# Order of products, activations and additions in the last convolutions of a four-block kernel

## What is computed

```python
def _L3_conv_ref(x, Wq, Wk, Wv, Wc, gamma, beta):
    q, k, v = conv3x3(x, Wq), conv3x3(x, Wk), conv3x3(x, Wv)
    att = softmax(einsum('nchw,mchw->nmhw', q, k) / sqrt(C), axis=1)
    virt = einsum('nmhw,mchw->nchw', att, v)
    mu, var = mean(virt, axis=(1, 2, 3)), var(virt, axis=(1, 2, 3))
    virt = (virt - mu) * rsqrt(var + 1e-05)
    virt = relu(virt * gamma + beta)
    return x + conv3x3(virt, Wc)
```

## Time and profile before

| | |
|---|---|
| Median of 3 executions | 482.8 us (481.6 to 485.68) |
| The profiled execution | 482.77 us, its span 481.0 us |
| Busy share of the span | PE 94%, DVE 71%, ACT 53%, POOL 26% |
| Granted TensorE clock, mean | 0.988 |
| Chain that ended last | PE 73%, DVE 10%, ACT 10%, issue 4%, DMA 2%, POOL 1% |

### The profile page before, as it was taken

How to read it: one execution, slowest core, us unless ns; L and a number is a source line. 1 busy time by engine, 2 the same in 40 slices (tenths; PEclk the granted TensorE clock), 3 DMA queues, 4 the chain that set the end, 5 groups by cost and what they waited for, 6 DMA issues and landing times.

```text
span 481.0 us, 10582 instructions
## 1 busy us (share of the span) xinstructions
PE 451.1 (94%) x3792; PEld 371.5 (77%) x3792; DVE 340.9 (71%) x891; ACT 254.6 (53%) x607; POOL 124.8 (26%) x154
## 2 busy tenths in 40 slices
PE   8898999899999999999999999999988999987995
PEld 7677775677887787778778877778766799887995
DVE  1567557976977897788778868986585344775995
ACT  4516737655646556575556565554654520494551
POOL 6115800351121012111210210121042011423662
PEclk9999999999999999999999999999995999999999
DMA  7210200030010001000200000000000000005111
GB/s 278 57 63 2 72 23 0 2 115 4 1 44 24 1 1 44 22 0 0 65 0 0 22 0 0 1 24 1 0 23 1 1 24 1 1 1 174 46 64 67
DMA packets 10639, 15.28 MB, mean 32 GB/s; under 512 B 624, under 2 KB 8944, under 8 KB 10480
## 3 DMA queue, kind: packets, MB, share of 16 engines
q1 hardware_dynamic: 10608, 14.86, 9.5%
HBM read 10.66 MB, written 4.19 MB: 31 GB/s over the span
## 4 chain that ended last, share of the span: by engine, by line
PE 73%; DVE 10%; ACT 10%; issue 4%; DMA 2%; POOL 1%; DVEq 0%; ACTq 0%; POOLq 0%
PE bank L1292 9%; PE bank L1293 8%; PE bank L1294 8%; PE bank L1529 6%; PE bank L1466 5%; PE bank L1312 4%; PE bank L1503 4%; PE bank L1501 2%; ACT prob L794 2%; PE bank L1557 2%; PE bank L1544 2%; PE bank L1430 2%; DMA x_t<-x_px 2%; PE bank L1516 2%; PE bank L1322 1%
## 5 line engine op out<-in xcount | busy, mean ns | idle before, releaser
L1292 PE MATMUL bank<-win,w_hi 128*128 128x256 f32 x360 | 108.4, 301 | 3.1 <-DVE win L1238 1.6
L794 ACT ACTIVATE prob<-bank 128x512 f32<-128x512 f32 x128 | 69.6, 597 | 63.0 <-PE bank L1501 62.0
L1293 PE MATMUL bank<-win,w_hi 128*128 128x256 f32 x360 | 101.4, 282 | 0.0
L1294 PE MATMUL bank<-win,w_lo 128*128 128x256 f32 x360 | 101.2, 281 | 0.0
L1064 DVE TENSOR_REDUCE nmax<-bank 128x2 f32<-128x512 f32 x128 | 84.3, 687 | 17.4 <-PE bank L1466 16.8
L1292 PEld LDWEIGHTS bank<-win,w_hi 128*128 128x128 f32 x360 | 67.9, 189 | 8.9 <-DVE win L1238 1.9
L1293 PEld LDWEIGHTS bank<-win,w_hi 128*128 128x128 f32 x360 | 68.1, 189 | 0.2
L1294 PEld LDWEIGHTS bank<-win,w_lo 128*128 128x128 f32 x360 | 67.8, 188 | 0.0
L583 POOL TENSOR_TENSOR first<-first 128x256 f32<-128x256 f32 x24 | 17.6, 732 | 146.4 <-ACT first L682 146.4
L1312 PE MATMUL bank<-ones_r 128*128 128x256 f32 x246 | 43.6, 310 | 1.1 <-DVE ones_r L900 1.1
L1503 PE MATMUL bank<-qk 32*128 32x256 f32 x256 | 40.8, 336 | 1.4 <-DVE q_max L1056 1.4
(11 more groups left out here) (276 smaller groups left out, 968.1 us busy)
## 6 DMA issues: line engine op xcount, KB each, us to landing
x_t<-x_px SPq DMA_DIRECT2D x8, 256.0 KB, 3.1
x_in<-x SPq DMA_DIRECT2D x8, 256.0 KB, 2.8
out<-x_pair SPq DMA_DIRECT2D x8, 256.0 KB, 2.2
q<-out SPq DMA_DIRECT2D x1, 2048.0 KB, 8.2
out<-v SPq DMA_DIRECT2D x8, 256.0 KB, 2.1
w_stage<-convs SPq DMA_DIRECT2D x3, 576.0 KB, 4.1
cst<-small SPq DMA_DIRECT2D x1, 1712.0 KB, 8.9
k<-convs SPq DMA_DIRECT2D x1, 576.0 KB, 4.0
```

The source lines that it names most:

```text
L794: act.activation(prob[:, x // 4 % 2, x % 4, :, :], bank[ST_BANK[x % 2]][:, :], ACT.Exp, scale=L2_SCALE).then_inc(st_exp, 1)
L1292: mm(dst, hi, x_hi, start=(row == 0), stop=False)
L1293: mm(dst, hi, x_lo, start=False, stop=False)
L1294: return mm(dst, lo, x_hi, start=False, stop=(row == KH - 1))
```

## The change

ACT's function `last_inputs` is split into `last_relu` (R) and `last_split` (S), and their order becomes R0 S0 R1, then R2 S1 R3 S2, R4 S3 R5 S4, R6 S5 R7 S6, then S7. On DVE the second group's factors come ahead of the low halves of pair 0, and the join's first three additions wait for the first group alone. On PE a pair's products are ordered anew: for both groups the 12 products with the high input parts (they wait for the split halves), then for both groups the 6 with the low parts (they wait for the low halves); `last_conv` now counts groups, not pairs. The last pair takes group 0 whole, high and low, and then group 1. Pairs 0, 1, 6 and 7 stand outside PE's loop. A bank's accumulation is started once, by its first product.

```diff
@@ -870,7 +870,7 @@
                     act.activation(virt[:, batch(a)], bank[6 + a % 2][:, :], ACT.Copy).then_inc(virt_copied, 1)
                     act.activation(sq3[a % 2], bank[6 + a % 2][:, :], ACT.Square).then_inc(sq3_done, 1)
 
-            def last_inputs(i, s):
+            def last_relu(i, s):
 
                 after(act, last_win, 4 * i + 2 * s - 2)
                 if isinstance(i, int) and i == 0:
@@ -880,7 +880,9 @@
                     act.activation(act3[s][:, m, :, :].rearrange("p h (t e) -> p h e t", e=2),
                                    tiled(virt)[:, bass.ds(n, 1), :, :].rearrange("p n (h e) t -> p (n h) e t", e=2),
                                    ACT.Relu, bias=lb[:, bass.ds(n, 1)], scale=la[:, bass.ds(n, 1)]).then_inc(act3_done, 1)
-                after(act, last_conv, 2 * i + s - 1)
+            def last_split(i, s):
+
+                after(act, last_conv, 4 * i + 2 * s - 2)
                 for h in range(2):
                     act.wait_ge(last_win, 4 * i + 2 * s + h + 1)
                     for m in range(2):
@@ -888,11 +890,15 @@
                                              windows3[s][:, 2 * h:2 * h + 2, m, :, :], ACT.Copy)
                     ins.then_inc(last_high, 1)
 
-            last_inputs(0, 0)
-            last_inputs(0, 1)
+            last_relu(0, 0)
+            last_split(0, 0)
+            last_relu(0, 1)
             with act.Fori(1, PAIRS // 2) as i:
-                last_inputs(i, 0)
-                last_inputs(i, 1)
+                last_relu(i, 0)
+                last_split(i - 1, 1)
+                last_relu(i, 1)
+                last_split(i, 0)
+            last_split(PAIRS // 2 - 1, 1)
 
 
         @block.vector
@@ -1249,12 +1255,13 @@
                 back = x3_back[:, cols].rearrange("p (m h t e) -> p e m h t", m=2, h=H, e=2)
                 even, odd = [y[:, cols].rearrange("p (m h t e) -> p e m h t", m=2, h=H, e=2)[:, e, :, :, :] for e in range(2)]
                 k = 4 * (2 * i + s)
-                dve.wait_ge(last_conv, 2 * i + s + 1)
+                dve.wait_ge(last_conv, 4 * i + 2 * s + 1)
                 dve.tensor_tensor(even, back[:, 0, :, :, :], m0, ALU.add).then_inc(last_chain, 1)
                 dve.tensor_tensor(odd, back[:, 1, :, :, :], m1, ALU.add).then_inc(last_chain, 1)
                 dve.wait_ge(last_chain, k + 1)
                 dve.tensor_tensor(even, even, m1, ALU.add).then_inc(last_chain, 1)
                 dve.wait_ge(last_chain, k + 2)
+                dve.wait_ge(last_conv, 4 * i + 2 * s + 2)
                 dve.tensor_tensor(odd, odd, m2, ALU.subtract).then_inc(last_chain, 1)
                 dve.wait_ge(last_chain, k + 3)
                 dve.tensor_tensor(even, even, m2, ALU.add).then_inc(y_done, 1)
@@ -1263,9 +1270,9 @@
 
             factors(0)
             last_windows(0, 0)
+            factors(1)
             first_low(0)
             first_low(1)
-            factors(1)
             last_windows(0, 1)
             dve.wait_ge(x3_back_in, 16)
             with dve.Fori(0, PAIRS // 2 - 1) as i:
@@ -1753,18 +1760,47 @@
             pe.wait_ge(w_split, 4)
             keep_busy(BUSY_NORM)
 
-            def last_convs(i):
-                for s in range(2):
-                    after(pe, y_done, 4 * i + 2 * s - 2)
-                    for g in range(2):
-                        pe.wait_ge(last_low, 4 * i + 2 * s + g + 1)
-                        for k in range(UNITS):
-                            ins = product(3, s, bank[2 * s + g][:, :], g, k)
-                    ins.then_inc(last_conv, 1)
-
-            last_convs(0)
-            with pe.Fori(1, PAIRS // 2) as i:
-                last_convs(i)
+            def last_product(s, g, k, part):
+
+                mix, row = 2 * g + k // KH, k % KH
+                o = POS[mix] * KC + row * C
+                x_hi, x_lo = [t[s][:, mix, :, row:row + H, :] for t in (win_hi, win_lo)]
+                dst = bank[2 * s + g][:, k // KH * HW:(k // KH + 1) * HW]
+                if part == "high":
+                    mm(dst, w3_hi[:, o:o + C], x_hi, start=(k == 0), stop=False)
+                    return mm(dst, w3_lo[:, o:o + C], x_hi, start=False, stop=False)
+                return mm(dst, w3_hi[:, o:o + C], x_lo, start=False, stop=(k == UNITS - 1))
+
+            def last_high_parts(i, s, g):
+
+                pe.wait_ge(last_high, 4 * i + 2 * s + g + 1)
+                for k in range(UNITS):
+                    last_product(s, g, k, "high")
+
+            def last_low_parts(i, s, g):
+
+                pe.wait_ge(last_low, 4 * i + 2 * s + g + 1)
+                for k in range(UNITS):
+                    ins = last_product(s, g, k, "low")
+                ins.then_inc(last_conv, 1)
+
+            def last_convs(i, s):
+                after(pe, y_done, 4 * i + 2 * s - 2)
+                for g in range(2):
+                    last_high_parts(i, s, g)
+                for g in range(2):
+                    last_low_parts(i, s, g)
+
+            last_convs(0, 0)
+            last_convs(0, 1)
+            with pe.Fori(1, PAIRS // 2 - 1) as i:
+                last_convs(i, 0)
+                last_convs(i, 1)
+            last_convs(PAIRS // 2 - 1, 0)
+            pe.wait_ge(y_done, 2 * PAIRS - 4)
+            for g in range(2):
+                last_high_parts(PAIRS // 2 - 1, 1, g)
+                last_low_parts(PAIRS // 2 - 1, 1, g)
 
 
 def constants():
```

## The result

The changed kernel takes 479.71 us (median of 13 executions, 478.55 to 481.68) against 482.8 before (13 executions): ratio 0.9923, 95% interval 0.9898 to 0.9947. The forecast was 479.5. The profiled execution took 480.18, its span 478.3 (before: 482.77 and 481.0).

A forecast was written before the change was run, and what follows sets the result against it. PE carries 73% of the chain, with DVE pacing the last stage. 482.77 less 3.20 (0.77 at the start, 1.44 of gaps, 0.99 at the end) is 479.57, rounded to 479.5 us; own range 479.0 to 480.0, with rivals 478.0 to 481.8.

The forecast's parts named there:

- The wait that decides: On PE, C2 needs J0, which stands behind W2 on DVE, so the price of W2 beside POOL decides.
- J0: DVE's join of pair 0, six additions; forecast to end at 447.5 us, 2.0 after W2.
- W2: DVE's windows step for pair 2; forecast to run from 442.18 to 445.5 us, beside POOL's four subtractions.
- C2: PE's products for pair 2; forecast to start at 447.68 us, let go by J0.
- C0: PE's products for pair 0, the last stage's first; forecast to start at 438.65 us.
- W2's length: On DVE, two instructions go before POOL starts, four each wait for a POOL instruction; POOL keeps its 2.83 us.
- the second rival: POOL and DVE block each other both ways in W2, J0 comes 0.9 us later: 480.5 us; chance 0.14.
- Who starts first: W2 starts on DVE at 442.18 us, ahead of POOL's low half at 442.4, and is blocked all the same.
- The start: On PE, with the high products first, C0 needs only the first split half and starts 0.77 us earlier.
- The pace: From C2 on, DVE's windows and joins set the stage's pace, 4.35 us a pair.
- The end: Three additions instead of six stand behind PE's last product, 0.99 us less.
- The cover: DVE's low halves come later, behind the moved factors; over 1.5 us of cover hide that, else at most 0.77 is lost.

The follow-up runs named there:

- e8: Changed kernel with POOL's low half of pair 1 subtracting one of 16 rows only; 476.83 us, executed once.
- e10: The changed kernel run once more without an edit; 480.08 us, ratio 0.9951 to the kernel before.
- e7: The kernel before with the new order of products alone; 484.13 us, ratio 1.0020.
- e2: Changed kernel with the second group's factors back behind the low halves of pair 0; 481.73 us, ratio 0.9973 to the kernel before.
- e11: Changed kernel with DVE's wait for the read-back moved behind W2, ahead of J0; 482.69 us, executed once.
- e3: Changed kernel with the old order of products in all pairs; 480.34 us, ratio 0.9958 to the kernel before.
- e4: Changed kernel with the last pair's products ordered like the others and the join waiting for both groups; 480.91 us, ratio 0.9958 to the kernel before.
- e1: Changed kernel with ACT's old order alone (R0 S0 R1 S1 R2 S2); 480.84 us, ratio 0.9943 to the kernel before.
- e9: Changed kernel with joins ahead of windows, 24 instead of 34 matmuls on ones, last group taken mix by mix; 480.01 us, ratio 0.9929 to the kernel before.

## Why the prediction was right

The wait that decides was named rightly, and so were the end and the size. Three smaller steps were wrong, and their errors nearly cancel.

- **The wait that decides.** The prediction named J0 behind W2, and W2's price beside POOL, as what sets C2. e8 shows the price (1.78 us). e10 shows that an earlier C0 counts for nothing: there C0 began 0.49 earlier than in the profile after and C2 0.02 later. A gap on PE was thus not worth its whole length, as the prediction's first paragraph had it; in e7 PE's first two gaps shrank and the stage stayed at 44.58.
- **W2's length.** Predicted were 3.32 (442.18 to 445.5), measured 3.33 and, in e10, 3.68; that two of them agree is luck. The end is what holds: 12.20 and 12.22, 0.3 after POOL's last subtraction and 0.36 later than predicted. Behind the 0.36 stand two errors. POOL didn't keep its 2.83: it took 3.45, pushed back by 0.62 by the lines that went between, which is the mechanism of the second rival (0.78 by its count). And POOL started 0.26 earlier than forecast, at 8.48 instead of 8.74, as DVE's factors and low halves between W0 and W1 took 1.96 and not 2.24. So the rival was right on the mechanism, and its 0.9 didn't come.
- **Who starts first.** The forecast let W2 start 0.22 ahead of POOL (442.18 and 442.4) and be blocked all the same. In e2 and e11 W2 did start so, 0.25 and 0.24 ahead, and wasn't blocked; the loss came in W3 instead, and e11's stage is 41.83. That W2 came second in the changed kernel is due to POOL's early start and to the read-back, which the prediction had as done by 441.6. The earlier trace rows shows that no byte moved from 441.5 to 442, but in the same trace the transfer has landed only at 441.91, and in the changed kernel W2 starts some 0.3 behind the landing. That POOL went first was therefore luck, worth 0.33 us by e11.
- **The start.** The 0.77 was measured (0.80 in e10 and e7), but in the profile after it was 0.31, at no cost. What the sum booked as 0.77 at the start and 1.44 of gaps, 2.21 in all, is one thing, J0's earlier end: C2 at 14.40 instead of 16.25, 1.85.
- **The pace.** Predicted were 4.35 a pair, set by DVE; it was 4.30, set by PE. DVE lost less in W3 (2.06) and W4 (2.25) than the 2.36 of before, since POOL's low halves beside them ended 0.80 and 1.00 after their start where it had been 1.09 and 1.06. That gave 0.24 over five pairs against the kernel before and made good most of the 0.36; that the two errors nearly cancel is luck. Of PE's 4.30, the pair behind C2's wait takes 4.37 and the others 4.28, where the old order takes 4.25 in e3: the new order costs 0.03 a pair, within the 0 to 0.05 that the prediction named and took as 0.
- **The end.** Predicted were 0.99, and e4 measured 0.90; C7 to the last product took 4.53 and three additions 1.08, as forecast.
- **The cover.** The factors that now come first were put down as covered by more than 1.5 us and as bringing R1 forward. e2 shows that this edit carries the largest part, 1.75, more than the factors' own time, because without it W2 and POOL change places.

Together, 1.85 of C2, 0.24 of the pace and 0.99 at the end are the 3.08 by which the stage is shorter. The parts undone one at a time cost 0.48, 1.75, 0.23 and 0.90, and the products alone bring nothing. They aren't independent: e1 acts through J0's end and then DVE's pace, e2 mostly through J1 and C3's wait of 1.18, e3 through PE's own way to C2, and only the end stands by itself.

## What to carry to other kernels

An earlier start is worth only what the next wait lets through: find the instruction behind which the second buffer comes free, and price that one first. Where two engines take turns, as POOL and DVE here, ask which of them will start first after the change and what the loser's lateness does to the next pass, for a wait that looks like loss can hold the better order. And where a stage is under a tenth of the span, measure it from a mark of its own, since what lies ahead may scatter by more than the change moves.

## What the runs showed that I had not expected

**Who comes first.** A difference of 0.3 us in W2's start turned the collision round. At 8.54 (e10) and 8.87 (the profile after), just behind POOL's 8.49 and 8.48, W2 took 3.68 and 3.33 and POOL 3.46 and 3.45. At 8.24 (e11), ahead of POOL, W2 took 1.49 and POOL 4.06, with one subtraction of 1.95 where the median is 0.73 to 0.76. DVE's instructions, which follow each other without a gap, kept POOL out for the whole of W2, not for one instruction. The Trainium skill, SBUF — State Buffer, section "Who interferes with whom", has the rule of which the prediction took only half: "Issue order, not op shape, decides who blocks." These runs agree with it.

**The clock.** In 9 of the 14 profiles the granted clock fell to 0.50 for some 3 us at the stage's start, in 5 it stayed at 1.00. The instructions ahead of the matmuls on ones are the same in all 14, among them the products on the sums with idle stretches of 0.57 and 0.95 us. In eight of the nine the fall began within 0.5 us of the stage's start and lay in the matmuls on ones: 34 of these then take 5.8 instead of 4.31 and cost C0 up to 0.5. In the ninth (e9) it lay in C0 and cost 1.51. What sets its moment wasn't tried.
